# Two attention layers on one core: outputs stored straight into SBUF, inverses spread by TensorE, maxima rows ahead of slot loads, output product steps in the last group

## What is computed

```python
# layer 0: 32 query heads of 16, one K/V head, no mask; gated FFN of width 1376
Q = xn @ Wq + bq; K = xn @ Wk + bk; V = xn @ Wv + bv
attn = softmax(einsum('bnhd,bkd->bhnk', Q, K) / 4)
x = x + einsum('bhnk,bkd->bnhd', attn, V) @ Wo + bo + (silu(xn @ G) * (xn @ U)) @ Wd
# layer 1: 32 query heads, 8 K/V heads, rotary embedding, causal mask;
# FFN: xn @ W_base.T + b_base + LoRA of the best 2 of 8 experts
x = x + softmax(causal(xq @ xk.T / 4)) @ xv @ Wo + ffn(xn)
```

## Time and profile before

| | |
|---|---|
| median of 3 runs | 2288.86 us (2284.86 to 2290.49) |
| profiled execution, its own time | 2291.59 us |
| its span | 2289.9 us |
| PE busy | 2002.2 us, 87% |
| DVE busy | 1434.8 us, 63% |
| ACT busy | 1090.0 us, 48% |
| mean granted clock | 0.91 |

### The profile page before, as it was taken

One profiled execution on the slowest core, in us unless ns is written; L12 is line 12 of the kernel. 1 busy time (PEld: TensorE's weight loads), 2 busy tenths in 40 slices (PEclk: granted clock), 3 DMA queues, 4 the chain that ended last, 5 costly groups with the idle time before them and its releaser, 6 DMA issues.

```text
span 2289.9 us, 28931 instructions
## 1 busy us (share of the span) xinstructions
PE 2002.2 (87%) x10608; PEld 990.4 (43%) x10608; DVE 1434.8 (63%) x1876; ACT 1090.0 (48%) x2150; POOL 227.9 (10%) x603
## 2 busy tenths in 40 slices
PE   3999999999999999999988868997888888886668
PEld 3878787633333333333332355444333333332216
DVE  7443445328888888888774183396666656664424
ACT  3221212234777777777664421142555555554460
POOL 4000000000000000000010030000231313131130
PEclk7999999997999999999896689996998989897889
DMA  5010100151121111113110211033111111112113
...
DMA packets 83297, 105.19 MB, mean 46 GB/s; under 512 B 18816, under 2 KB 52608, under 8 KB 83168
## 3 DMA queue, kind: packets, MB, share of 16 engines
...
...
## 4 chain that ended last, share of the span: by engine, by line
PE 68%; DVE 10%; ACT 8%; SPq 6%; DMA 5%; issue 2%; POOL 0%; DVEq 0%; POOLq 0%; ACTq 0%
PE ps L1165 17%; PE ps L1194 11%; ACT arena L666 6%; PE ps L955 6%; PE ps L956 6%; PE ps L957 6%; PE ps L1190 6%; PE ps L1112 5%; PE ps L1073 4%; PE ps L1118 3%; DMA slots<-arena 3%; PE ps L1029 2%; DVE arena L891 2%; SPq L353 2%; SPq L350 2%
## 5 line engine op out<-in xcount | busy, mean ns | idle before, releaser
L891 DVE TENSOR_REDUCE arena<-ps 128x1 f32<-128x1024 f32 (+7 forms) x1024 | 976.4, 988 | 323.1 <-PE ps L1115 225.8
L666 ACT ACTIVATE arena<-ps 128x512 f32<-128x512 f32 (+3 forms) x1792 | 874.2, 555 | 526.2 <-PE ps L1190 293.2
L1165 PE MATMUL ps<-arena 128*17 128x512 f32 (+3 forms) x3584 | 455.2, 581 | 22.5 <-ACT arena L657 21.9
L1194 PE MATMUL ps<-slots 50*128 50x512 f32 x1024 | 397.2, 473 | 29.7 <-ACT arena L666 10.9
L1118 PE MATMUL ps<-slots 48*128 48x512 f32 x1024 | 414.4, 484 | 8.1 <-DVE arena L891 7.2
L1194 PEld LDWEIGHTS ps<-slots 50*128 50x128 f32 x1024 | 177.5, 195 | 351.4 <-ACT arena L666 280.1
L1190 PE MATMUL ps<-slots 98*128 98x512 bf16 (+3 forms) x768 | 230.5, 356 | 87.9 <-DMA slots<-arena 84.6
L1112 PE MATMUL ps<-slots 96*128 96x512 bf16 (+3 forms) x768 | 231.9, 361 | 20.2 <-DVE arena L891 7.0
L955 PE MATMUL ps<-x_hi,w_hi 128*128 128x512 f32 (+1 forms) x480 | 195.4, 407 | 56.9 <-DVE x_lo L921 35.7
L1118 PEld LDWEIGHTS ps<-slots 48*128 48x128 f32 x1024 | 174.5, 195 | 60.5 <-DVE arena L891 34.2
L523 POOL TENSOR_SCALAR_AFFINE_SELECT arena<-arena 128x128 f32<-128x128 f32 x512 | 146.9, 294 | 497.8 <-ACT arena L666 486.2
...
## 6 DMA issues: line engine op xcount, KB each, us to landing
...
numer<-arena SPq DMA_DIRECT2D x256, 32.0 KB
...
```

Of the source, the lines that this page charges most:

```text
L666: act.activation(prob[local % P_RING][:, q0:CH], bank(local % SP_RING)[:, q0:CH], ACT.Exp, scale=SCALE).then_inc(S["p_ready"], 1)
L891: dve.tensor_reduce(maxes[c][:, h * TPC + qt:h * TPC + qt + 1], src[:, 0:max_width(l == 1, c, qt)], AX_X, ALU.max).then_inc(S["x_done"], 1)
L1165: mm = pe.matmul(bank(7)[32 * h:32 * h + DH + 1, q0:CH], v_slot[n % SLOTS][:, kt, :], prob[idx % P_RING][:, q0:CH], start=(kt == 0), stop= ...
L1194: mm = pe.matmul(bank(slot)[:, q0:CH], k_slot[u][r:r + ROWS[0] + MROWS, kt * P:(kt + 1) * P].bitcast(F32R), q_slot[u][r:r + ROWS[0] + MROW ...
```

## The change

- SP issues the maxima rows of the second half before the slot load.
- `store_o` writes each head's 16 rows straight into `xnT` and its denominators, as 4 rows of 128, into `inv`, both in SBUF: eight DMAs per half. The DRAM buffers, `load_output` and `load_inverses` go.
- The inverses are spread by PE: `sel` is a matrix of zeros and ones, and `broadcast` is four fp32 products of 32 rows by 128 columns. For batch 0 these are eight items in the stream of maxima of block 14 (worked in group 13), each followed by DVE's product; DVE's reciprocal moves to block 12. For batch 1 they stand in the order of the output product (`tail_ring`).
- The output product is a list of 72 steps (a quarter tile, or one `broadcast`) over four banks. In the last group three steps follow each quad, from the eighth quad in layer 0 and the third in layer 1 on, at most 28 in all; the rest follows the group. In the last group of layer 0 the maxima are spread over the first 0.42 of it.
- ACT splits `Wo` in group 10 and batch 0's outputs in group 14, POOL makes their low parts. DVE's moments are a function of their own; layer 1's transposes take four banks and its first routing products stand between them; the FFN, projection and rotary loads of layer 1 are issued earlier.

```diff
+LAST_MAX_END = [0.42, 0.0]
 AHEAD = [6, NX]
+FIRST_PROJ = [7, 2]
+STEPS_PER_QUAD = 3
+O_BYTES = 128
...
-        blocks.append(r[0][:2] + before + r[0][2:] + r[1][:2] + [(n, 0, None, None)] + r[1][2:])
+        norms = [(None, c, None, k) for c in range(QC) for k in range(KC)] if n == GROUPS - 2 else []
+        blocks.append(r[0][:2] + before + norms + r[0][2:] + r[1][:2] + [(n, 0, None, None)] + r[1][2:])
...
+def norms_through():
+    items = [item for block in max_blocks() for item in block]
+    return items.index((None, QC - 1, None, KC - 1)) + 1
+def tail_ring():
+    norms = [[("norm", c, k) for k in range(KC)] for c in range(NCH)]
+    tiles = [("tile", t // TPC, t) for t in range(TT)]
+    return tiles[0:6] + norms[2] + tiles[6:9] + norms[3] + tiles[9:TT]
...
+                b = n // NG
                 for h in range(HG):
-                    sp.dma_start(numer[l][n * HG + h:n * HG + h + 1, :, c * CH:(c + 1) * CH].rearrange("o d q -> (o d) q"),
+                    head = n % NG * HG + h
+                    r = head % (P // DH) * DH
+                    sp.dma_start(xnT[r:r + DH, head // (P // DH), b * N + c * CH:b * N + (c + 1) * CH],
                                  o_sb[c][32 * h:32 * h + DH, :]).then_inc(S["o_out"][c], 16)
-                sp.dma_start(denom[l][n * HG:(n + 1) * HG, c * CH:(c + 1) * CH],
-                             o_sb[c][DH:P:32, :]).then_inc(S["o_out"][c], 16)
+                    sp.dma_start(inv[head * TPC:(head + 1) * TPC, b * QC + c, :],
+                                 o_sb[c][32 * h + DH:32 * h + DH + 1, :].rearrange("o (a q) -> o a q", q=P)).then_inc(S["o_out"][c], 16)
...
-                    if n == GROUPS - 4:
-                        load_output(l, 0)
-                    if n == GROUPS - 2:
-                        load_inverses(l, 0)
-                    final = n == GROUPS - 1
+                    max_rows(l, u, 1, n * QC + 1)
                     if n + SLOTS - 1 < GROUPS:
                         sp.wait_ge(S["pv_done"], n * group_quads[l] + PQ)
...
-                    if not final:
+                    if n < GROUPS - 1:
                         max_rows(l, v, 0, (n + 1) * QC)
                     store_o(l, n, 1)
-                load_output(l, 1)
-                load_inverses(l, 1)
...
+                    if l == 0 and n == 2:
+                        sp.wait_ge(S["acc_biased"], TT)
+                        sp.dma_start(bias_o[:, :], bbase.partition_broadcast(P)).then_inc(bias_in[1], 16)
+                        sp.wait_ge(S["q_ready"], NCH * NQ)
+                        load_projections(1)
+                    if l == 0 and n == GROUPS - 4:
+                        sp.wait_ge(S["wo_ready"], 1)
+                        load_output_weight(1)
...
+                    sp.wait_ge(L[0]["o_copied"], GROUPS * QC + 1)
+                    load_ffn1()
                     sp.wait_ge(L[0]["y2_ready"], TT)
-                    sp.wait_ge(L[0]["y2_evac"], TT)
-                    load_projections(1)
-                    load_ffn1()
-                if l == 1:
-                    sp.wait_ge(S["b_ready"], TT)
...
+                def low(c):
+                    pool.wait_ge(S["xo_hi_done"], KC * (c + 1))
+                    pool.tensor_tensor(xo_lo[:, c % 2, :, :], xnT[:, :, c * CH:(c + 1) * CH], xo_hi[:, c % 2, :, :].bitcast(F32),
+                                       ALU.subtract).then_inc(S["xo_ready"], 1)
                 at = 0
                 for n in range(GROUPS):
                     for c in range(QC):
+                        if (n, c) == (GROUPS - 5, 0):
+                            pool.wait_ge(S["wo_hi_done"], KC)
+                            pool.tensor_tensor(wo_lo[:, :, :], w_o[:, :, :], wo_hi[:, :, :].bitcast(F32), ALU.subtract).then_inc(S["wo_ready"], 1)
+                        if (n, c) == (GROUPS - 2, 1):
+                            low(0)
+                            if l == 0:
+                                pool.wait_ge(S["pv_done"], n * group_quads[l] + PQ)
+                                low(1)
+                        if l and (n, c) == (GROUPS - 1, 1):
+                            pool.wait_ge(S["pv_done"], n * group_quads[l] + PQ)
+                            low(1)
...
+                def xo_high(c, k):
+                    if c < QC:
+                        act.wait_ge(S["x_done"], norms_through())
+                    else:
+                        act.wait_ge(S["on_ready"], (c - QC) * KC + k + 1)
+                        act.wait_ge(S["y2_ready"], (c - 1) * TPC)
+                    act.activation(xo_hi[:, c % 2, k, :], xnT[:, k, c * CH:(c + 1) * CH], ACT.Copy).then_inc(S["xo_hi_done"], 1)
...
-                        act.wait_ge(S["o_out"][c], n * 80 + 16)
+                        act.wait_ge(S["o_out"][c], (n + 1) * O_BYTES)
...
+                                if n == GROUPS - 6 and c == 0 and h == 0:
+                                    if kt == 0:
+                                        act.wait_ge(S["wo_in"], 16)
+                                    if kt < KC:
+                                        act.activation(wo_hi[:, kt, :], w_o[:, kt, :], ACT.Copy).then_inc(S["wo_hi_done"], 1)
+                                if n == GROUPS - 2 and h == 0 and halves < 2 * KC:
+                                    xo_high(*divmod(halves, KC))
+                                    halves += 1
...
+                for c in range(QC, NCH):
+                    for k in range(KC):
+                        xo_high(c, k)
+                    if l == 0 and c == QC:
...
+                    if n is None:
+                        o = xnT[:, h, c * CH:(c + 1) * CH]
+                        dve.tensor_tensor(o, o, src[:, 0:CH], ALU.mult).then_inc(S["x_done"], 1)
+                        return
...
+                def invert(c0, c1, groups):
+                    for c in range(c0, c1):
+                        dve.wait_ge(S["o_out"][c % QC], (groups + 1) * O_BYTES)
+                    dve.reciprocal(inv[:, c0:c1, :], inv[:, c0:c1, :]).then_inc(S["inv_ready"], 1)
...
-                    if n == GROUPS - 2:
-                        invert(0)
+                    if n == GROUPS - 4:
+                        invert(0, QC, NG)
...
+                def norm(c):
+                    for k in range(KC):
+                        r = ring.index(("norm", c, k))
+                        dve.wait_ge(S["norm_ready"], (c - QC) * KC + k + 1)
+                        o = xnT[:, k, c * CH:(c + 1) * CH]
+                        dve.tensor_tensor(o, o, bank(3 + r % 4), ALU.mult).then_inc(S["on_ready"], 1)
...
+                def evac(t0, t1):
+                    for t in range(t0, t1):
+                        src = bank(3 + ring.index(("tile", t // TPC, t)) % 4)
+                        dve.wait_ge(S["y2_ready"], t + 1)
+                        if l == 0:
+                            dve.tensor_tensor(acc[:, t, :], acc[:, t, :], src, ALU.add).then_inc(S["y2_evac"], 1)
+                        else:
+                            if t >= 8:
+                                dve.wait_ge(S["stored"][t % 8], 16)
+                            dve.tensor_tensor(res[t % 8], acc[:, t, :], src, ALU.add).then_inc(S["y2_evac"], 1)
...
+                dve.wait_ge(S["pv_done"], (GROUPS - 1) * group_quads[l] + PQ)
+                evac(0, 4)
+                chunk_moments(0)
+                evac(4, 6)
+                invert(2, 3, GROUPS)
+                norm(2)
+                low(2)
+                invert(3, 4, GROUPS)
+                evac(6, 9)
+                norm(3)
+                evac(9, 10)
+                low(3)
+                evac(10, 12)
+                chunk_moments(1)
+                if l == 0:
+                    normalise(1, 0)
+                chunk_moments(2)
+                if l == 0:
+                    normalise(1, 1)
+                evac(12, 16)
+                if l == 0:
+                    normalise(1, 2)
+                chunk_moments(3)
+                if l == 0:
+                    normalise(1, 3)
...
+                    def lora_in(g):
+                        for t in range(g * TPC, (g + 1) * TPC):
+                            pe.wait_ge(S["xnT_ready"], t + 1)
+                            if t < 4:
+                                pe.wait_ge(L[0]["y2_evac"], TT)
+                            else:
+                                pe.wait_ge(S["hl_sb"], t - 3)
+                            for k in range(KC):
+                                last = pe.matmul(bank(3 + t % 4)[:, 0:E * R + E], xnT[:, k, t * P:(t + 1) * P], w_ar[:, k, :],
+                                                 start=(k == 0), stop=(k == KC - 1))
+                            last.then_inc(S["hl_ready"], 1)
...
+                    for t in range(3 * TPC):
+                        transpose_x(t)
...
+                    lora_in(0)
+                    for t in range(3 * TPC, TT):
+                        transpose_x(t)
+                    for g in range(1, NCH):
```

(54 more changed lines are left out.)

203 lines of the change are left out of this document (75 added, 128 removed).

## The result

The changed kernel takes 2172.48 us, median of 4 runs (2162.25 to 2190.96), against 2286.86 for the kernel before (4 runs): ratio 0.951, 95% interval 0.944 to 0.958. It is faster, but by 114 us and not by the 183 forecast, and it lies above the range of 2072 to 2152. A second set of four runs of it gave 2170.47. The profiled execution has a span of 2173.4 us, 66.5 above the forecast's span of 2106.9.

What follows compares the result with a forecast made beforehand. TensorE was taken to bound the kernel, with stalls by the DMA queue. Gains of 63.5 us in layer 0 and 119.5 in layer 1, together 183.0, took 2291.59 to 2108.6, so 2106 as median; own range 2085 to 2130, wider 2072 to 2152.

Steps and rivals of the forecast that it cites:

- part 3: Both layers' group 13: inverses spread by TensorE, eight items per layer, cost 8.3 us each layer.
- part 5: Last groups with output-product steps: layer 0 takes 54 us, 26 gained; layer 1 takes 38 to 40, 7.5 longer.
- part 7: After layer 1's last PV: 34.9 us to the end instead of 70.4, 35.5 us gained.
- rival b: Clock stays down in a last group, or layer 1's attention swings: 2120 to 2143 us, chance 0.15.
- group 13 longer by over 12 us: A listed sign that the forecast is wrong, in the group that holds the broadcast items.
- Part 1: Layer 1's attention: maxima ahead of the slot load remove 82.2 us of waits, plus 20 us from pipeline drain and clock.
- Rival (a): Layer 1's maxima stay late behind the eight-DMA store, 2 us of each wait staying: 2154 us, chance 0.12.
- Parts 2, 4, 6: Layer 0: batch 0 loads removed, 11.7 us gained; copies moved into attention, 3.6 lost; after last PV, 37.7 gained.
- The rule weighed: Short idles between PSUM-cycling products may swing the clock; then layer 1's 20 us would not come, giving 2126 us.
- (c): More than forecast: layer 1's groups fall to 30 us instead of 32, broadcasts cost half: 2076 us, chance 0.10.
- (d): Slower than before: slot loads behind the maxima come late; 6 us of wait per group would cancel all, chance 0.03.
- (e): Queue order does not matter because maxima are ready late anyway: 2208 us, chance 0.03.

Runs made afterwards that it cites:

- f3_no_items: The changed kernel with batch 0's eight broadcast items left out in both layers, its heads left unnormalised; 2118.6 us, ratio 0.927.
- e4_maxima_first: The kernel before with only the second chunk's maxima rows issued ahead of the slot load; 2207.1 us, ratio 0.966.
- f2_rows_first: The changed kernel with the next group's second-chunk maxima rows issued, in layer 1, ahead of the second chunk's store; 2159.8 us, ratio 0.945.
- f4_all_three: The changed kernel with items spread at no pace cost, last-group steps one behind each score, and layer 1's maxima rows ahead of the store; 2148.2 us, ratio 0.939.
- h3_best: The changed kernel with batch 0's inverses spread by DMA, layer 1's maxima rows ahead of the store, last-group steps behind the second score; 2089.3 us, ratio 0.913.

## Why the prediction was wrong

The sum first: of the 66.5 us over the forecast's span, the items of part 3 hold 35.0 in layer 0 (43.3 against 8.3) and 9.2 in layer 1 (17.5 against 8.3); layer 1 without items holds 21.1 (748.5, where the parts give 819.7 - 102.2 + 2.4 + 7.5 = 727.4). The rest is 1.2. Of the 21.1, the waits hold 15 (17.1 in f3_no_items, against 2) and the last group 8 (47.1 against 39); the other terms brought 2 more than forecast. Two slips in the sums are small: a quad's terms in part 5 add up to 4.0 and not 3.95, those of part 7 to 34.7 and not 34.9.

- **Part 3, inverses by TensorE: the step that failed.** I priced the products by the nearest row and took "8.3 each" for a layer, with 1.6 an item as the upper bound. The duration was nearly right (1.20 at full clock, the first item of the changed kernel). What failed was to add it as work beside a stream in which a score and a maximum run at the same time on different rows, and in which each item stands in the place of a maximum. The group took 86.8 us in the profiled execution where it takes 43.8 without items: 43 us and not 8.3. No bound of mine held a clock at 0.50 for a whole group. I had asked where the clock falls only for the last groups (rival b); it fell in group 13. The prediction did name "group 13 longer by over 12 us" as a sign of being wrong, and it came. That where the items stand and at what pace sets the price in layer 0 is shown (11.5, 21.2, 29 to 43 us for the same work); why the clock falls is not.
- **Part 1, maxima ahead of the slot load: right, one term mis-sized.** The queue order was the cause (e4_maxima_first), and removing a us of wait took off more than a us, as said. "Eight take some 3.5 us, if the one-row ones are as long" became 4.9, and the 2 us of rest became 16.8, which f2_rows_first takes away. Rival (a) named that condition, with 2 us left per wait; 0.95 to 2.9 were left.
- **Part 5, last group.** Layer 0: the clock stays at 1.00, as said, but the group took 65.8 us and not 54: 4.87 us a quad instead of 3.95, for the changes of shape and the wait for a score's bank. Layer 1: 46.9 us from its first score at 2091.3 to the copy at 2138.2, where 39 were forecast; behind the second score the same steps make it 41.8. The clock did fall in last groups of other runs (f4_all_three, to 0.83 over the group), so that part of rival (b) is not idle.
- **Parts 2, 4, 6.** Without the items, stretch 0 is 69.4 us shorter than before; the parts gave 68.5 in it (8.4 - 3.6 + 26 + 37.7). By pieces, in f3_no_items: 13.6 us gained up to the last group's first score (106.1 before, 92.5 now; 4.8 forecast; in the kernel before the clock was at 0.51 for some 14 us from 1130 and 7 from 1188, and the copies of part 4 cost nothing visible), 14.1 in the last group (26), 41.6 after the last copy (37.7). The near agreement of the sum is luck: it hides terms that missed in opposite ways.
- **Part 7.** 35.2 us from the last copy to the end, 34.9 forecast.
- **The rule weighed.** The Trainium skill (TensorE: Matmul & The Clock Gate, A second HAM failure mode: psum-queue depth-cycling) tells of a kernel whose clock swings because TensorE idles briefly between groups of products that cycle through PSUM banks. Carried over to this kernel, it would have had the clock swing in layer 1 and part 1's 20 us stay away. The traces do not show it here: h3_best hands over to ScalarE at every score and has 1.00 over 550 us, with TensorE busy for 468 of the 498 us to 2048, and e4_maxima_first won more than the wait it removed.
- **(c), (d) and (e)** did not occur: the group period is 32.9 us in ordinary groups, 32 forecast, and 31.9 in f2_rows_first, where no wait is left; no wait for a slot's load appears; the maxima were not late anyway.
